# An attention and feed-forward layer on one Trainium2 core: rounds of two score pairs, and part of the softmax exponentials on VectorE

## The chip, the cores and the metric

The kernel runs on one core of one Trainium2 chip. Its engines are TensorE (PE in the profile; PEld is its weight load), ScalarE (ACT), VectorE (DVE), GpSimd (POOL) and SyncE (SP), which issues DMAs. The metric is the device time of one execution in microseconds (us), lower is better.

## The reference

The input is 4096 tokens of width 256. What is computed, cut to what matters:

```python
h = _layernorm(x) * (1 + ca) + sa
q = einsum('bnhd,hed->bnhe', h by 16 heads of 16, Wq)
attn = softmax(einsum('bnhe,bmhe->bhnm', q, q) / NORM)      # 16 heads of 4096 x 4096, NORM = 0.25
x = x + ga * (einsum('bhnm,bmhe->bnhe', attn, q) @ Wp.T + bp)
h = _layernorm(x) * (1 + cb) + sb
# feed-forward: a layer norm of its own, 256 -> 1024, silu, 1024 -> 256, dequantised weights
x = x + gb * _L0_ffn_ref(h, ...)                             # h + 0.5 * z
```

All scores are exponentiated: 16 x 4096 x 4096 of them.

## The kernel before

**Two stages.** The start stage (some 82 us) normalises the tokens, computes q, writes it to DRAM in two 16-bit parts and derives a shift for the softmax. The attend stage is nearly all of the time, and the change lies there.

**Tiling.** A block of tokens is 512 query tokens (eight blocks, `c`). A group is one block with 4 heads (four groups per block, 32 in all, `gg`). In a group there are 64 score pairs: 16 steps (`j`) by 4 heads, where a pair is two key tiles of 128 against the 512 queries. TensorE writes the scores of a pair, 128 x 1024, into one of three PSUM slots (`S_RING`); ScalarE takes their exp in one instruction (L744) and writes it into one of 12 buffers `probs` (`P_RING`). A score pair may be written when the exp of three pairs before has been done (semaphore `exps_done`).

**Weighing.** A unit is one key tile of four heads: four matmuls side by side of the `probs` against `values` (L788, function `weigh`), added up in the PSUM bank `ps_sums`. A group has 32 units. The matmuls of a unit are fp32 and are recorded as eight, in two passes of four. When a group is done, VectorE copies the sums (`copy_sums`, L927), TensorE turns them (`turn_sums`, L802), and VectorE divides (`divide`, L933 and L938). The first unit of the next group waits for that division (`group_done`).

**Output stage.** From group 4 on, TensorE also works on the block of tokens before: 44 pieces of work for a block (`out_piece`), 11 in each group: turning the attention result, the projection, turning the normalised tokens, the layer up (`up`, two pieces for each of 8 tiles of the hidden layer) and the layer down. All of them go through the one PSUM bank `ps_out`. After some pieces VectorE empties the bank (`after_piece`: `take_att`, `residual`, `take_z2`, `take_up` at L991, `finish_y`), and the next piece waits for it. A tile of the hidden layer needs a tanh on ScalarE (L729) and one more pass on VectorE (L995, `finish_hidden`). The two layer norms of a block run on VectorE in one go (`first_norm`, `second_norm`) while TensorE has no pieces that need them. GpSimd adds the bias to the tokens (L708) and makes the base of the output (L715 to L719).

**Order.** The order on each engine is written by hand. TensorE works in rounds (`SIZES`): ten of three score pairs, one of two, and again, 22 in a group. After the scores of a round come one or two units (`UNITS`), and in every second round one piece (`PLACE_ROUND`), so that a round holds two blocks of fp32 work: two units, or a unit and a piece. At a group's start, round 0 weighs the last two units of the group before and round 1 turns its sums. SyncE reloads a ring of four quarters of keys as each is used up.

## Time and profile before

| | us |
|---|---|
| median of 3 runs | 2074.18 (2073.5 to 2074.28) |
| the profiled execution | 2074.52 |
| its span, first to last instruction | 2072.7 |
| TensorE busy | 1958.2 |
| ScalarE busy | 1966.9 |
| VectorE busy | 377.8 |
| GpSimd busy | 70.4 |
| mean granted clock of TensorE | 0.993 |

The span is 1.8 us shorter than the profiled execution's own time, which is within 0.4 us of the median. A matmul's end in the profile is modelled and matmuls are pipelined, so a matmul's duration is longer than what it adds; what it adds is read from start to start. The same holds for ScalarE, whose instructions overlap a little. "issue" in a row is time without a wait that the profile shows.

### The profile page before, as it was taken

The numbers are of one execution on the slowest core, as the hardware profiler recorded it, in microseconds if no ns is written. First come the engines' busy times: TensorE is split into PE (matmuls) and PEld (weight loads), VectorE is DVE, ScalarE is ACT, GpSimd is POOL, SyncE is SP. The second block draws the span as 40 slices with busy tenths as digits, with TensorE's granted clock in tenths as the row PEclk, the third lists the DMA queues.
The fourth block names the chain that finished last, engine by engine and source line by source line (L and its number), as shares of the span: only waits on it lengthen the run. The fifth ranks groups of instructions, "written<-read, shape, count | busy, mean of one in ns | idle before, by whom it ended". The sixth has DMA issues, their size and how long they took to land.

```text
span 2072.7 us, 42098 instructions
## 1 busy us (share of the span) xinstructions
PE 1958.2 (94%) x18325; PEld 533.5 (26%) x18325; DVE 377.8 (18%) x903; ACT 1966.9 (95%) x2174; POOL 70.4 (3%) x35
## 2 busy tenths in 40 slices
PE   5888889999999999999999999999999999999997
PEld 4311112222222222222222222222222222222224
DVE  7310002210031100410022100311004100231004
ACT  3899999999999999999999999999999999999982
POOL 0000000100010000100001000100001000010000
PEclk9999999999999999999999999999999999999998
DMA  5541111211111221111211111111111112111100
GB/s 160 150 124 46 35 50 41 51 51 42 55 38 48 51 50 51 46 45 41 56 46 50 51 43 53 37 49 51 51 51 45 46 41 56 46 41 41 31 12 12
DMA packets 121337, 108.05 MB, mean 52 GB/s; under 512 B 21936, under 2 KB 120112, under 8 KB 120896
## 3 DMA queue, kind: packets, MB, share of 16 engines
q1 hardware_dynamic: 120400, 103.69, 18.8%
q8 instruction: 144, 2.36, 0.5%
q10 hardware_dynamic: 752, 1.67, 0.2%
q14 instruction: 41, 0.34, 0.1%
HBM read 96.49 MB, written 8.65 MB: 51 GB/s over the span
## 4 chain that ended last, share of the span: by engine, by line
ACT 46%; PE 42%; issue 7%; DVE 1%; ACTq 0%; DVEq 0%
ACT attend_probs L744 45%; PE attend_sums L788 21%; PE attend_scores L776 13%; PE attend_out L796 6%; PE attend_scores L796 1%; PE attend_out L802 1%; PE attend_sums L802 1%; ACT attend_half_tanh L729 1%; ACT attend_ffn_in L753 0%; PE attend_scores L802 0%; DVE attend_st L1085 0%; DVE z L1097 0%; DVE attend_rsqrt_work L91 0%; DVE attend_rsqrt_work L93 0%; DVE attend_rs L95 0%
## 5 line engine op out<-in xcount | busy, mean ns | idle before, releaser
L744 ACT ACTIVATE attend_probs<-attend_scores 128x1024 f32<-128x1024 f32 x2048 | 1891.6, 1038 | 18.6 <-PE attend_scores L776 18.6
L788 PE MATMUL attend_sums<-attend_probs,values 128*17 128x512 f32 x8192 | 1011.2, 597 | 0.0
L776 PE MATMUL attend_scores<-asks,keys 64*128 64x512 f16 x4096 | 673.3, 384 | 74.1 <-ACT attend_probs L744 57.4
L776 PEld LDWEIGHTS attend_scores<-asks,keys 64*128 64x128 f16 x4096 | 150.9, 94 | 886.0 <-ACT attend_probs L744 817.2
L788 PEld LDWEIGHTS attend_sums<-attend_probs,values 128*17 128x17 f32 x8192 | 171.3, 96 | 392.4 <-issue 337.3
L796 PE MATMUL attend_out<-w,hidden 128*32 128x256 f32 x1920 | 124.2, 379 | 0.0
L796 PE MATMUL attend_out<-attend_ffn_in,w 128*32 128x512 f32 x896 | 116.6, 592 | 0.0
L927 DVE COPY attend_sums_sb<-attend_sums 128x512 f32<-128x512 f32 x32 | 22.2, 692 | 487.4 <-PE attend_sums L788 487.4
L991 DVE TENSOR_SCALAR attend_half_in<-attend_out,b_col 128x512 f32<-128x512 f32 x56 | 42.0, 751 | 333.4 <-PE attend_out L796 332.4
L796 PEld LDWEIGHTS attend_out<-w,hidden 128*32 128x32 f32 x1920 | 62.0, 110 | 86.3 <-issue 64.2
L1001 DVE TENSOR_TENSOR base<-attend_out,base 128x512 f32<-128x512 f32 x14 | 9.7, 691 | 376.6 <-PE attend_out L796 376.6
L995 DVE SCALAR_TENSOR_TENSOR hidden<-attend_half_tanh,attend_half_in 128x512 f32<-128x512 f32 x56 | 38.8, 692 | 158.7 <-ACT attend_half_tanh L729 158.7
L715 POOL TENSOR_TENSOR base<-attend_hid,mod 128x1024 f32<-128x1024 f32 x7 | 16.6, 2368 | 1030.3 <-DVE attend_hid L977 1030.3
L708 POOL TENSOR_TENSOR attend_x_now<-attend_x_now,bp_ga 128x1024 f32<-128x1024 f32 x8 | 19.1, 2385 | 815.3 <-DMA attend_x_now<-L_attn_x 667.8
L796 PEld LDWEIGHTS attend_out<-attend_ffn_in,w 128*32 128x32 f32 x896 | 28.8, 110 | 59.9 <-issue 59.9
L729 ACT ACTIVATE attend_half_tanh<-attend_half_in 128x512 f32<-128x512 f32 x56 | 36.1, 644 | 0.0
L950 DVE TENSOR_TENSOR attend_x<-attend_out,attend_x_now 128x512 f32<-128x512 f32 x15 | 10.4, 691 | 140.9 <-PE attend_out L796 140.9
L802 PE MATMUL attend_sums<-ident,attend_sums_sb 128*32 128x128 f32 x1024 | 34.6, 276 | 0.8 <-DVE attend_sums_sb L927 0.8
L337 ACT ACTIVATE start_h_feat<-start_ps,mod_col 128x512 f32<-128x512 f32 x16 | 11.5, 773 | 22.8 <-PE start_ps L385 22.8
L796 PE MATMUL attend_out<-wp,attend_att_feat 128*32 128x256 f32 x480 | 31.2, 379 | 0.0
L753 ACT ACTIVATE attend_ffn_in<-attend_scores,beta_col,gamma_col 128x256 f32<-128x256 f32 x4 | 2.0, 560 | 29.6 <-PE attend_scores L796 29.6
L802 PEld LDWEIGHTS attend_sums<-ident,attend_sums_sb 128*32 128x32 f32 x1024 | 26.0, 109 | 8.8 <-DVE attend_sums_sb L927 8.8
(140 smaller groups left out, 548.2 us busy)
## 6 DMA issues: line engine op xcount, KB each, us to landing
keys<-parts_dram SPq DMA_DIRECT2D x768, 64.0 KB
keys<-parts_dram SPq DMA_DIRECT2D x256, 56.0 KB
asks<-parts_dram SPq DMA_DIRECT2D x192, 64.0 KB
start_x_in<-L_attn_x SPq DMA_DIRECT2D x8, 512.0 KB, 9.5
parts_dram<-start_q_parts SPq DMA_DIRECT2D x16, 256.0 KB, 2.5
attend_x_now<-L_attn_x SPq DMA_DIRECT2D x8, 512.0 KB, 4.3
out<-base SPq DMA_DIRECT2D x16, 256.0 KB, 2.7
asks<-parts_dram SPq DMA_DIRECT2D x64, 56.0 KB
```

Source lines behind the costliest of these rows:

```text
L337: last = act.activation(h_feat[:, g % 2, k, :], ps_turn[:, k, :], ACT.Identity, bias=mod_col[:, k:k + 1], scale=mod_col[:, 2 + k:3 + k])
L708: pool.tensor_tensor(x_now, x_now, wide(bp_ga[:, :]), ALU.add).then_inc(xb_ready, 1)
L715: pool.tensor_tensor(base, hid, wide(mod[:, 3, :]), ALU.mult).then_inc(base_step, 1)
L729: act.activation(half_tanh[:, f % 2, :], half_in[:, f % 2, :], ACT.Tanh).then_inc(tanh_done, 1)
L744: act.activation(probs[n % P_RING], ps_scores[:, 2 * slot:2 * slot + 2, :], ACT.Exp, scale=scale)\
L776: last = pe.matmul(ps_scores[:, 2 * (n % S_RING) + b, :], keys[rows, part % K_RING, hq, col:col + P], asks[rows, group * Q_HEADS + hq, :], ...
L788: last = pe.matmul(ps_sums[32 * hq:32 * hq + E1, :], values[:, j + STEPS * b, (gg % Q_GROUPS) * Q_HEADS + hq, :], probs[n % P_RING][:, b, ...
L796: last = pe.matmul(to[32 * q:32 * q + 32, :], held[:, 32 * q:32 * q + 32], moved, start=start, stop=stop)
L802: last = pe.matmul(bank[32 * q:32 * q + 32, t * P:(t + 1) * P], source(t)[:, 32 * q:32 * q + 32], ident[:, :], start=True, stop=True)
L927: dve.tensor_copy(sums_sb, ps_sums).then_inc(sums_copied, 1)
L991: dve.tensor_scalar(half_in[:, f % 2, :], ps_out, b1_col[:, f:f + 1], 0.5, ALU.add, ALU.mult).then_inc(half_ready, 1)
L995: dve.scalar_tensor_tensor(out=hidden[:, f, :], in0=half_tanh[:, f % 2, :], scalar=1.0, in1=half_in[:, f % 2, :], op0=ALU.add, op1=ALU.mul ...
```

## The change

**TensorE.** Rounds now have two score pairs each, 32 in a group. A round has one unit (rounds 9 and 21 have two, rounds 0 and 1 one each of the group before, rounds 2 and 3 none) and, in 22 of the 32 rounds, half a piece: half the query columns of the layer up, one tile of the hidden layer in the layer down, half of the tiles in a turn, one half of the contraction in the projection. The work in matmuls is the same. The sums are turned in round 2, the new group's weighing starts in round 4.

**Exps on VectorE.** In every seventh round (every fifth in the first four groups, with some left out) the first pair is a pair that lies 12 places ahead, and its exp is computed by VectorE in seven passes over 128 x 1024 (`exp_of`): the scores times 2^23/ln 2 as an integer, its fraction and its power of two by bit operations, and a product of two polynomials. It is written into one of two buffers `exps`. The passes are put into four rounds in a row: 0 and 1, then 2 and 3, then 4 and 5, then 6. The score slot is free after pass 0 (semaphore `taken`). That is 23 pairs in the first four groups and 114 in the other 28, 137 of 2048.

**GpSimd's work** goes to VectorE: four passes over 128 x 1024 for each block (`add_bias`, one in `second_norm`, `finish_base`). To make room in SBUF, `x_now` and `hid` share the space of `x1` and `z1`; the load of the next tokens is issued in the last quarter but one of a block's last group, after `finish_base`.

```diff
-SIZES = [3] * 10 + [2] + [3] * 10 + [2]
-ENDS = [sum(SIZES[:r + 1]) for r in range(len(SIZES))]
-STARTS = [0] + ENDS[:-1]
-UNITS = [0, 0] + [2 - r % 2 for r in range(2, len(SIZES))]
-WEIGHED = [sum(UNITS[:r + 1]) for r in range(len(SIZES))]
-PLACE_ROUND = range(1, len(SIZES), 2)
+ROUND = 2
+ROUNDS = PAIRS // ROUND
+LATE = 2
+UNITS = [0] * 4 + [2 if r in (9, 21) else 1 for r in range(4, ROUNDS)]
+WEIGHED = [sum(UNITS[:r + 1]) for r in range(ROUNDS)]
+PLACE_ROUND = [r for r in range(2, ROUNDS) if r % 4 != 1][:22]
...
+LEAD, E_RING = 12, 2
+def vector_round(gg, r):
+    if gg < Q_GROUPS:
+        return (ROUNDS * gg + r) % 5 == 0 and (gg != 1 or r < 15)
+    busy = gg % Q_GROUPS == 0 and 15 <= r <= 28
+    return (ROUNDS * gg + r) % 7 == 0 and not busy
+def emission():
+    order, by_vector, taken, following = [], [], set(), 0
+    for gg in range(GROUPS):
+        for r in range(ROUNDS):
+            for i in range(ROUND):
+                early = len(order) + LEAD
+                if i == 0 and vector_round(gg, r) and early < GROUPS * PAIRS and early not in taken:
+                    order.append(early)
+                    by_vector.append(True)
+                    taken.add(early)
+                    continue
+                while following in taken:
+                    following += 1
+                order.append(following)
+                by_vector.append(False)
+                taken.add(following)
+    return order, by_vector
+ORDER, BY_VECTOR = emission()
+PLACE = {n: e for e, n in enumerate(ORDER)}
+TURN = [sum(BY_VECTOR[:e]) if BY_VECTOR[e] else e - sum(BY_VECTOR[:e]) for e in range(len(ORDER))]
+SCALAR_PAIRS = [n for n, v in zip(ORDER, BY_VECTOR) if not v]
+VECTOR_PAIRS = [n for n, v in zip(ORDER, BY_VECTOR) if v]
...
+TURN_ATT, PROJECT, TURN_Z2, UP, DOWN = 0, 2, 10, 12, 28
...
+                dve.tensor_scalar(log2_scale, exp_scale, 2.0 ** 23 / math.log(2.0), None, ALU.mult).then_inc(scale_set, 1)
...
+        hid = z2 = z1[:, :, :]
...
+            eng.dma_start(x1, x_v[:, o * GT:(o + 1) * GT, :]).then_inc(xn_in, 16)
...
-                    if within == 8 and c > 0:
-                        sp.wait_ge(x1_ready, 2 * c)
+                    if within == 14 and c > 0:
+                        sp.wait_ge(base_step, 3 * c)
...
-            @block.gpsimd
...
-                    pool.tensor_tensor(x_now, x_now, wide(bp_ga[:, :]), ALU.add).then_inc(xb_ready, 1)
...
+                        if not BY_VECTOR[e]:
+                            turn, slot = TURN[e], e % S_RING
+                            act.wait_ge(scores_ready, e + 1)
+                            if turn >= P_RING:
+                                act.wait_ge(steps_done, SCALAR_PAIRS[turn - P_RING] // Q_HEADS + 1)
+                            act.activation(probs[turn % P_RING], ps_scores[:, 2 * slot:2 * slot + 2, :], ACT.Exp, scale=scale)\
+                               .then_inc(exps_done, 1)
...
+                    if e >= S_RING:
+                        pe.wait_ge(taken if BY_VECTOR[e - S_RING] else exps_done, TURN[e - S_RING] + 1)
...
+                        wait(pe, vector_exps, before(VECTOR_PAIRS, gg * PAIRS + Q_HEADS * (j + 1)))
...
+                def up(f, k, half, bank):
+                    cols = slice(half * D, (half + 1) * D)
+                    last = by_columns(bank[:, cols], w1[:, k, f * P:(f + 1) * P], ffn_in[:, k, cols], k == 0, k == DC - 1)
+                    if k == DC - 1 and half == 1:
...
-                    for r in range(len(SIZES)):
-                        for p in range(STARTS[r], ENDS[r]):
-                            scores(gg, p)
-                        if r == 0 and gg > 0:
-                            for unit in range(WEIGHED[-1], 2 * STEPS):
-                                weigh(gg - 1, unit)
-                        if r == 1 and gg > 0:
-                            turn_sums(gg - 1)
+                    for r in range(ROUNDS):
+                        for p in range(ROUND * r, ROUND * r + ROUND):
+                            scores(gg * PAIRS + p)
+                        if r < LATE and gg > 0:
+                            weigh(gg - 1, WEIGHED[-1] + r)
                         for unit in range(WEIGHED[r] - UNITS[r], WEIGHED[r]):
                             weigh(gg, unit)
                         if r in PLACE_ROUND and c > 0:
-                            out_piece(c - 1, group * SLOTS + r // 2)
+                            out_half(c - 1, group * SLOTS + PLACE_ROUND.index(r))
+                        if r == LATE and gg > 0:
+                            turn_sums(gg - 1)
...
+                def add_bias(o):
+                    dve.wait_ge(xn_in, 16 * (o + 1))
+                    dve.tensor_tensor(x1, x1, wide(bp_ga[:, :]), ALU.add).then_inc(xb_ready, 1)
+                def finish_base(o):
+                    dve.wait_ge(base_step, 3 * o + 1)
+                    dve.tensor_tensor(base, base, wide(b2_gb[:, :]), ALU.add).then_inc(base_step, 1)
+                    dve.wait_ge(base_step, 3 * o + 2)
+                    dve.tensor_tensor(base, base, x1, ALU.add).then_inc(base_step, 1)
+                def exp_of(d, i):
+                    e = PLACE[VECTOR_PAIRS[d]]
+                    slot, values_out = e % S_RING, exps[d % E_RING].rearrange("p b n -> p (b n)")
+                    power_f = power.bitcast(F32)
+                    if i == 0:
+                        dve.wait_ge(scores_ready, e + 1)
+                        wait(dve, exp_scaled, d)
+                        if d == 0:
+                            dve.wait_ge(scale_set, 1)
+                        dve.tensor_scalar(power, ps_scores[:, 2 * slot:2 * slot + 2, :].rearrange("p b n -> p (b n)"),
+                                          log2_scale, -120.0 * 2.0 ** 23, ALU.mult, ALU.max).then_inc(taken, 1)
+                    elif i == 1:
+                        dve.wait_ge(taken, d + 1)
+                        wait(dve, vector_exps, d)
+                        dve.tensor_scalar(fraction.bitcast(I32), power, 0x007FFFFF, 0x3E800000,
+                                          ALU.bitwise_and, ALU.bitwise_or).then_inc(power_step, 1)
+                    elif i == 2:
+                        dve.wait_ge(power_step, 4 * d + 1)
+                        dve.tensor_scalar(power, power, 0x7F800000, FACTOR,
+                                          ALU.bitwise_and, ALU.bitwise_xor).then_inc(power_step, 1)
+                    elif i == 3:
+                        dve.wait_ge(power_step, 4 * d + 2)
+                        if d >= E_RING:
+                            dve.wait_ge(steps_done, VECTOR_PAIRS[d - E_RING] // Q_HEADS + 1)
+                        dve.scalar_tensor_tensor(out=values_out, in0=fraction, scalar=A1 * 2.0 ** -2, in1=fraction,
+                                                 op0=ALU.add, op1=ALU.mult).then_inc(power_step, 1)
+                    elif i == 4:
+                        dve.wait_ge(power_step, 4 * d + 3)
+                        dve.scalar_tensor_tensor(out=fraction, in0=fraction, scalar=B1 * 2.0 ** -2, in1=fraction,
+                                                 op0=ALU.add, op1=ALU.mult).then_inc(power_step, 1)
+                    elif i == 5:
+                        dve.wait_ge(power_step, 4 * d + 4)
+                        dve.scalar_tensor_tensor(out=fraction, in0=fraction, scalar=B0 * 2.0 ** -4, in1=power_f,
+                                                 op0=ALU.add, op1=ALU.mult).then_inc(exp_scaled, 1)
+                    elif i == 6:
+                        dve.wait_ge(exp_scaled, d + 1)
+                        dve.scalar_tensor_tensor(out=values_out, in0=values_out, scalar=A0 * 2.0 ** -4, in1=fraction,
+                                                 op0=ALU.add, op1=ALU.mult).then_inc(vector_exps, 1)
...
-                    if gg > 0:
-                        copy_sums(gg - 1)
-                        divide(gg - 1)
-                    if gg == 1:
-                        weights()
-                    if gg == 2:
-                        gate_weights()
-                    if c > 0:
-                        for s in range(group * SLOTS, (group + 1) * SLOTS):
-                            after_piece(c - 1, s)
-                            after_tanh(c - 1, s)
+                    for r in range(ROUNDS):
+                        now = ROUNDS * gg + r
+                        if r - 1 in PLACE_ROUND and c > 0:
+                            h = group * SLOTS + PLACE_ROUND.index(r - 1)
+                            if h % 2 == 1:
+                                after_piece(c - 1, h // 2)
+                        if BY_VECTOR[ROUND * now]:
+                            begun_at[now] = begun
+                            begun += 1
+                            for i in (0, 1):
+                                exp_of(begun_at[now], i)
+                        if r == LATE and gg > 0:
+                            copy_sums(gg - 1)
+                        if r == LATE + 1 and gg > 0:
+                            divide(gg - 1)
+                        for ago, steps in ((1, (2, 3)), (2, (4, 5)), (3, (6,))):
+                            if now - ago in begun_at:
+                                for i in steps:
+                                    exp_of(begun_at[now - ago], i)
+                        if r - 3 in PLACE_ROUND and c > 0:
+                            h = group * SLOTS + PLACE_ROUND.index(r - 3)
+                            if h % 2 == 1:
+                                after_tanh(c - 1, h // 2)
+                        if (gg, r) == (1, 18):
+                            weights()
+                        if (gg, r) == (1, 24):
+                            gate_weights()
+                        if (group, r) == (0, 5) and c > 0:
+                            add_bias(c - 1)
+                        if (group, r) == (2, 13) and c > 0:
+                            finish_base(c - 1)
...
+                add_bias(G - 1)
```

**TensorE, inside a token block's layer up.** Before; L776 scores, L788 a unit, L796 a piece:

```order
L776 MATMUL attend_scores<-asks,keys 128x512 [waits exps_done]
L776 MATMUL attend_scores<-asks,keys 128x512
L776 MATMUL attend_scores<-asks,keys 128x512 [waits exps_done]
L776 MATMUL attend_scores<-asks,keys 128x512
L776 MATMUL attend_scores<-asks,keys 128x512 [waits exps_done]
L776 MATMUL attend_scores<-asks,keys 128x512
L788 MATMUL attend_sums<-attend_probs,values 17x512 x4
L796 MATMUL attend_out<-attend_ffn_in,w 32x512 [waits half_ready]
L796 MATMUL attend_out<-attend_ffn_in,w 32x512 x3
L776 MATMUL attend_scores<-asks,keys 128x512 [waits exps_done]
```

and of the changed kernel (L826 scores, L839 a unit, L847 half a piece; `attend_exps` is a pair of VectorE's):

```order
L826 MATMUL attend_scores<-asks,keys 128x512 [waits exps_done]
L826 MATMUL attend_scores<-asks,keys 128x512
L826 MATMUL attend_scores<-asks,keys 128x512 [waits exps_done]
L826 MATMUL attend_scores<-asks,keys 128x512
L839 MATMUL attend_sums<-attend_exps,values 17x512 [waits vector_exps,exps_done]
L839 MATMUL attend_sums<-attend_probs,values 17x512 x3
L847 MATMUL attend_out<-attend_ffn_in,w 32x256 [waits half_ready]
L847 MATMUL attend_out<-attend_ffn_in,w 32x256 x3
L826 MATMUL attend_scores<-asks,keys 128x512 [waits exps_done]
L826 MATMUL attend_scores<-asks,keys 128x512
L826 MATMUL attend_scores<-asks,keys 128x512 [waits exps_done]
L826 MATMUL attend_scores<-asks,keys 128x512
```

The piece has become two of 256 columns, in two rounds, and each stands behind two pairs and one unit.

**VectorE, at the start of group 10**, where the sums are copied and divided. Before:

```order
L995 SCALAR_TENSOR_TENSOR hidden<-attend_half_tanh,attend_half_in 128x512
L927 COPY attend_sums_sb<-attend_sums 128x512
L933 RECIPROCAL attend_inverse<-attend_sums 128x16
L938 TENSOR_TENSOR attend_att<-attend_sums,attend_inverse 128x4x64
L991 TENSOR_SCALAR attend_half_in<-attend_out,b_col 128x512
```

and of the changed kernel, where L1065 and L1070 are passes 0 and 1 of an exp and L985 is the copy of the sums:

```order
L1106 SCALAR_TENSOR_TENSOR hidden<-attend_half_tanh,attend_half_in 128x512
L1065 TENSOR_SCALAR attend_power<-attend_scores,gains 128x1024
L1070 TENSOR_SCALAR attend_fraction<-attend_power 128x1024
L985 COPY attend_sums_sb<-attend_sums 128x512
L991 RECIPROCAL attend_inverse<-attend_sums 128x16
L996 TENSOR_TENSOR attend_att<-attend_sums,attend_inverse 128x4x64
L1074 TENSOR_SCALAR attend_power<-attend_power 128x1024
L1080 SCALAR_TENSOR_TENSOR attend_exps<-attend_fraction 128x1024
L1084 SCALAR_TENSOR_TENSOR attend_fraction<-attend_fraction 128x1024
L1088 SCALAR_TENSOR_TENSOR attend_fraction<-attend_fraction,attend_power 128x1024
```

Two passes of an exp, which wait for scores of round 2, now stand ahead of the copy, and the other five behind the division.

## Rows read from the trace of the kernel before

**Rows 1.** Page, part 1: busy time, share of the span and instructions of each engine.

```profile
PE 1958.2 (94%) x18325; PEld 533.5 (26%) x18325; DVE 377.8 (18%) x903; ACT 1966.9 (95%) x2174; POOL 70.4 (3%) x35
```

**Rows 2.** Busy time per stretch: groups 1 to 3, then groups 4 to 7.

```profile
core 0: us, PE busy (x) PEld busy (x) DVE busy (x) ACT busy (x) POOL busy (x), PEclk, DMA share, GB/s
143.50:319.70 176.20, 156.93 (x1248) 34.17 (x1248) 14.73 (x23) 176.20 (x194) 2.49 (x1) 1.00 0.17 45
319.70:561.70 242.00, 235.91 (x2242) 61.27 (x2242) 39.69 (x86) 239.79 (x266) 9.51 (x4) 1.00 0.18 47
```

**Rows 3.** Timeline, PE: a round with one unit and a piece (start us, us).

```profile
1004.67 0.99 PE L776 MATMUL attend_scores<-asks,keys 64*128 64x512 f16 x6
1005.59 1.05 PE L788 MATMUL attend_sums<-attend_probs,values 128*17 128x512 f32 x8
1006.46 1.05 PE L796 MATMUL attend_out<-w,hidden 128*32 128x256 f32 x16
1007.44 0.60 PE L776 MATMUL attend_scores<-asks,keys 64*128 64x512 f16 x4
```

**Rows 4.** Timeline, PE: second of three score pairs in that round.

```profile
1004.90 0.38 PE L776 MATMUL attend_scores<-asks,keys 64*128 64x512 f16 x2
```

**Rows 5.** Timeline, PEld: third score pair and unit of that round.

```profile
1005.27 0.10 PEld L776 LDWEIGHTS attend_scores<-asks,keys 64*128 64x128 f16 x2 [0.48 <-ACT attend_probs L744]
1005.59 0.13 PEld L788 LDWEIGHTS attend_sums<-attend_probs,values 128*17 128x17 f32 x8 [0.23 <-issue]
```

**Rows 6.** Timeline, PE: a group boundary, sums turned.

```profile
1047.85 1.14 PE L776 MATMUL attend_scores<-asks,keys 64*128 64x512 f16 x6
1048.91 1.08 PE L802 MATMUL attend_sums<-ident,attend_sums_sb 128*32 128x128 f32 x32
1049.81 1.06 PE L802 MATMUL attend_out<-ident,attend_att 128*32 128x128 f32 x32
```

**Rows 7.** Timeline, ACT: an exp, a tanh and the next exp.

```profile
448.30 1.03 ACT L744 ACTIVATE attend_probs<-attend_scores 128x1024 f32<-128x1024 f32 x1
449.20 0.64 ACT L729 ACTIVATE attend_half_tanh<-attend_half_in 128x512 f32<-128x512 f32 x1
449.72 1.03 ACT L744 ACTIVATE attend_probs<-attend_scores 128x1024 f32<-128x1024 f32 x1
```

**Rows 8.** Timeline, ACT: an exp that came after an idle wait for its scores.

```profile
501.80 1.02 ACT L744 ACTIVATE attend_probs<-attend_scores 128x1024 f32<-128x1024 f32 x1 [0.44 <-PE attend_scores L776]
```

**Rows 9.** Timeline, PE: the scores that it waited for.

```profile
501.37 0.82 PE L776 MATMUL attend_scores<-asks,keys 64*128 64x512 f16 x6
```

**Rows 10.** Timeline, DVE: sums copied and divided at that boundary.

```profile
1047.98 0.69 DVE L927 COPY attend_sums_sb<-attend_sums 128x512 f32<-128x512 f32 x1 [1.90 <-PE attend_sums L788]
1050.06 0.26 DVE L933 RECIPROCAL attend_inverse<-attend_sums 128x16 f32<-128x16 f32 x1 [1.39 <-PE attend_sums L802]
1050.35 0.42 DVE L938 TENSOR_TENSOR attend_att<-attend_sums,attend_inverse 128x256 f32<-128x256 f32 x1
```

**Rows 11.** Groups by line, DVE: operations like the added ones (mean ns).

```profile
L991 DVE TENSOR_SCALAR attend_half_in<-attend_out,b_col 128x512 f32<-128x512 f32 x56 | 42.0, 751 | 333.4 <-PE attend_out L796 332.4
L977 DVE TENSOR_TENSOR attend_hid<-attend_hid,mod 128x1024 f32<-128x1024 f32 x7 | 8.6, 1226 | 0.2
```

**Rows 12.** Groups by line, DVE, 60 to 420 us: SBUF to SBUF, constant operands.

```profile
L1029 DVE TENSOR_SCALAR z<-mod 128x512 f32<-128x512 f32 x1 | 0.4, 415 | 0.0
```

**Rows 13.** Timeline, DVE: two passes after each other, and the second norm's end.

```profile
835.97 0.69 DVE L950 TENSOR_TENSOR attend_x<-attend_out,attend_x_now 128x512 f32<-128x512 f32 x1 [9.80 <-PE attend_out L796]
842.35 1.23 DVE L975 TENSOR_TENSOR attend_hid<-z,mod 128x1024 f32<-128x1024 f32 x1
843.61 1.23 DVE L977 TENSOR_TENSOR attend_hid<-attend_hid,mod 128x1024 f32<-128x1024 f32 x1
853.65 1.38 DVE L981 TENSOR_SCALAR z<-attend_hid,attend_mo,attend_rs 128x256 f32<-128x256 f32 x4
```

**Rows 14.** Timeline, DVE: in its first work of the attend stage.

```profile
83.59 0.68 DVE L1033 TENSOR_TENSOR z<-z,mod 128x512 f32<-128x512 f32 x1
```

168 lines of the change are left out of this document (85 added, 83 removed).

## The prediction

> **What bounds the kernel now.** I read the page's busy times first: ScalarE 95%, TensorE 94% [rows 1]. With two engines that near to full, shares decide nothing, and the stretches come next. Groups 1 to 3, without an output stage, take 176.2 us for 192 score pairs, or 0.918 a pair: ScalarE is busy all of it, TensorE for 156.93, so ScalarE is the bound. A token block with the output stage (groups 4 to 7) takes 242.0 us, 60.5 a group, and there TensorE is busy for 235.91 and ScalarE for 239.79 [rows 2]. So in 28 of 32 groups TensorE is nearly as late as ScalarE, and each engine has to be costed from start to start, since durations overlap.
>
> *TensorE.* From one score pair to the next 0.23 [rows 3, 4]. From the last pair of a round to the unit 0.32 [rows 5], so going over to fp32 work costs 0.09. A unit takes 0.87 (1005.59 to 1006.46). From the piece to the next scores 0.98; the piece itself has as many columns as a unit, 0.86, so going back costs 0.12 [rows 3]. Each round thus pays 0.21 for changing over and back, whatever lies between. A turn of the sums takes 0.90 [rows 6]. A group's own work, before: 64 x 0.23 = 14.7, 32 units at 0.87 = 27.8, 11 pieces at 0.86 = 9.5, the turn 0.9, and 22 rounds x 0.21 = 4.6: **57.5 us** of 60.5.
>
> *ScalarE.* 0.90 from an exp to the next when its work is ready, 0.52 for a tanh between two exps [rows 7]. A group with two tanhs: 64 x 0.90 + 2 x 0.52 = 58.6; the remaining 1.9 are waits for scores or buffers such as the 0.44 of [rows 8].
>
> **The change, part by part.**
>
> *Rounds of two.* The same matmuls, but 32 rounds: ten more changes over and back, 10 x 0.21 = **+2.1**. TensorE's own work becomes **59.6 us** a group; it was 60.5 in all. That TensorE pays for the change of form and not for the size of the blocks is what these rows show. The Trainium skill has a rule that speaks against this change (TensorEngine Tiling (Array Packing), Key Properties): changing the tiling mode drains the engine, changing the tile alone does not. Scores use the array in two halves of 64 rows and the fp32 work in groups of 32 columns. By that rule the 0.21 is a drain that comes each time; were it only the latency of a wait, TensorE's own work would be 57.5 less 4.6, whatever the rounds, which is the third rival.
>
> *Exps taken from ScalarE.* 114 pairs in 28 groups, 4.1 a group: 4.1 x 0.90 = 3.7 less, ScalarE's own 58.6 becomes 54.9. From group 4 on this buys at most the way down to TensorE's 59.6: 60.5 - 59.6 = 0.9 a group. **ScalarE stops being the bound, TensorE becomes it**, and every wait of TensorE then counts in full.
>
> *What an exp costs on VectorE.* Pass 0 reads PSUM: 0.75 for 512 elements, and 512 more cost 1.23 - 0.69 = 0.54 [rows 10, 11], so 1.29. Passes 1 and 2 have one source in SBUF and constants: 0.415 for 512 [rows 12], twice that less the fixed 0.16, so 0.67. No row shows a bit operation of that size; the upper end is 1.23, that of a two-source pass, and I take 0.67, the nearer row. Passes 3 to 6: 1.23 each [rows 11]. 0.03 between dependent passes [rows 13]. Passes 0-1: 1.99; 2-3: 1.96; 4-5: 2.52; 6: 1.26: **7.7 us in a row**, of some 13 us between two such exps, so VectorE has the time but not at every moment. The skill (VectorE: DVE Perf Modes, What auto-detection actually checks) lets the operands decide on the faster mode and not the operation; by it, 0.67 too, and only if that fails here 1.23.
>
> Pass 0 starts as an exp does, 0.43 after its scores [rows 8, 9], so passes 0-1 end 2.42 after the start of the round. A full round is 0.23 + 0.32 + 0.87 + 0.43 + 0.12 = 1.96, one without half a piece 1.53.
>
> *The copy of the sums.* It began 0.13 after the next scores (1047.98, 1047.85) and lasts 0.69 [rows 6, 10]; with 0.06 to reach TensorE it ends 0.88 into round 2, and the turn is due at 0.23 + 0.32 + 0.43 = 0.98. The spare is 0.10. An exp of VectorE comes every seven rounds, so one always lies near the boundary, by round:
> - 2: passes 0-1 stand ahead of the copy, free at 2.42: TensorE waits 2.2
> - 1: 2.42 - 1.53 = 0.89: waits 0.7
> - 0: with passes 2-3, 4.38 - 3.06 = 1.32: 1.1
> - 31: with passes 4-5, 6.90 - 4.59 = 2.31: 2.1
> - 30: with pass 6, 8.16 - 6.55 = 1.61: 1.4
> - 3: the copy is in time, but the division (0.26 + 0.42) stands behind passes 0-1 and ends at 3.2; round 4's unit wants it at 1.10 + 0.55: 1.6
> - 29: 0.
>
> The mean of the seven is **1.3 a group**. Queued behind the waiting turn or unit are all scores, so ScalarE starves behind it.
>
> *The bank `ps_out`.* After an emptying piece VectorE's pass (0.69 to 0.75) is done 0.94 into the next round and wanted at 1.42. If the exp began three rounds before, passes 4-5 end at 6.90 - 5.88 = 1.02, the pass at 1.86: a wait of 0.4, and 0.9 with a short round among the three; at two or four rounds 0.3 to 0.4, only with short rounds. Over the seven positions 0.2 for each of some 14 such places in a block: 2.8, or **0.7 a group**.
>
> *Other waits.* The score slot: passes 0-1 begun at 0.43, `taken` at 1.78, wanted 0.23 into the next round, 2.19, or 1.76 behind a short round, later when `take_up` stands ahead: 0.2. ScalarE: in rounds 29, 31, 0, 1, 5 TensorE needs 1.53 and in round 3 only 1.10, against 1.80 for two exps, and a tanh adds 0.52, so TensorE waits for exps there; between 0 and 2.5, and I take 0.7, since VectorE's exp or a wait above often falls on the same rounds.
>
> From group 4 on: 59.6 + 1.3 + 0.7 + 0.2 + 0.7 = 62.5, against 60.5: **+2.0 x 28 = +56 us**; nothing of it lies beside other work, as TensorE is the path.
>
> *The first four groups.* TensorE's own work there is 59.6 - 9.5 = 50.1 and ScalarE stays the bound: 23 pairs x 0.918 = -21. Against it: an exp every five rounds (nine of ScalarE's, 8.3 us) leaves 0.6 beside the 7.7, three boundaries cost some 2 each, and the first pair of all goes to VectorE, which was still on its first work at 83.59 [rows 14], some 2 to 3 late. **-12 us.**
>
> *At nothing.* GpSimd's work moved: 4 x 1.23 = 4.9 a block on VectorE, in rounds without an exp near it except `finish_base` (2.5), which can delay a `taken` by 1 once in several blocks. The norms ran from 835.97 to 855.0 [rows 13], 19 us, within 11 rounds of at least 1.9; one pass more still fits. SyncE's load waits for `finish_base`, two thirds of a group earlier; stores and keys behind it have 30 us. The tail and the start stage keep their chains (+0.2 for one small pass).
>
> **The sum.** 2074.5 + 56 - 12 = 2118.5. The terms of the waits were taken one by one though they partly fall together, which takes off a little: **2116 us**, 2% slower.
>
> **The rivals.**
>
> *VectorE is never late* (a wait falls where ScalarE would have made TensorE wait anyway). Then 59.6 + 0.9 = 60.5 from group 4 on, no change, and the first groups give 21 less some 4: some 2056, and with the waits for ScalarE at half, 2045. For it: VectorE is 18% busy and gets 137 x 7.5 = 1030 us more, half of the span. Against: the copy's spare of 0.10. It would need the boundary waits below 0.5 a group. Faster.
>
> *The bit operations take the slow mode*: 1.12 more in each chain, 8.8 of 8.3 us available in the first groups (VectorE is the bound there, +12), and each case above later by 0.56 to 1.12: +1.2 at the boundary and in `ps_out` together: +34. Some 2162. Against: the rows of the same form.
>
> *The changes over and back are hidden*: then TensorE's own work is 52.9, ScalarE stays the bound with 54.9 and waits of about 2.5, so 57.5: -3.0 x 28 - 12, some 1978. Against: the 0.32 and 0.98 stand in rounds where TensorE was not held.
>
> *The change doesn't do what it says*: ScalarE's exps would still be 2048. The order on the engines excludes it.
>
> **Chances.** The forecast 0.64 (2085 to 2145), VectorE in time or nearly so 0.20 (2040 to 2085, of which 0.14 lies below 2070 and 0.04 within 0.2% of before), slow bit operations 0.10, changes hidden 0.04, others 0.02. 0.2%, 4 us, is about what a measurement of this kernel can tell from no change. Faster 0.18, same 0.06, slower 0.76. The range of 2050 to 2145 leaves out the slow bit operations, the hidden changes and the lowest part of the second case, some 0.2.
>
> **What the profile would show.** TensorE: 1.95 to 1.97 from round to round and 0.32 ahead of each unit. The exps on ScalarE: 1911, with idle time ahead of them that names scores. Waits of TensorE that name VectorE: the turn for the copy (some 1 us a group), `ps_out` work for L1102, scores for L1065. VectorE's passes: 1.29, 0.67, 0.67, 4 x 1.23. Groups 1 to 3 at 54 to 56 us, later ones at 62 to 63. I am wrong if the later groups take 60.5 or less, which would mean that the waits for VectorE fall together with those for ScalarE, or that a round costs TensorE less than 1.96.

## The result and the profile after

The changed kernel takes 2242.66 us (median of 4 runs, 2242.02 to 2244.17) beside 2073.84 of before: **8.2% slower**, ratio 1.0815 with an interval of 1.0796 to 1.0834. The direction was as forecast, the size was not: 169 us lost instead of 42.

The page of the changed kernel (columns as in [rows 1]):

```profile
PE 1969.9 (88%) x19221; PEld 512.3 (23%) x19221; DVE 1385.0 (62%) x1885; ACT 1890.4 (84%) x2038; POOL 1.3 (0%) x6
```

No engine is near full: TensorE has gone from 94% to 88%, ScalarE from 95% to 84%. GpSimd is empty, VectorE at 62%. VectorE computes 136 exps (x136 in its rows below; ScalarE's are x1912 of 2048), one fewer than the 137 that the section on the change and the prediction give. A token block with the output stage, groups 4 to 7 (columns as in [rows 2]):

```profile
core 0: us, PE busy (x) PEld busy (x) DVE busy (x) ACT busy (x) POOL busy (x), PEclk, DMA share, GB/s
326.50:587.20 260.70, 237.09 (x2372) 58.83 (x2368) 159.07 (x204) 231.26 (x248) 0.00 (x0) 1.00 0.17 44
```

It takes 260.7 us where it took 242.0 [rows 2], 65.2 a group. TensorE is busy for as long as before (237.09 against 235.91); what has been added is idle time of TensorE. Who it waited for, from the waits of the changed kernel (line waited: us in total, times, longest):

```profile
PE attend_sums L839 <- ACT attend_probs L788: 162.5, 179, 1.8
PE attend_sums L853 <- DVE attend_sums_sb L985: 19.6, 22, 1.9
PE attend_sums L839 <- DVE attend_exps L1092: 8.3, 1, 8.3
PE attend_scores L826 <- DVE attend_power L1065: 7.1, 12, 3.3
PE attend_sums L839 <- DVE attend_att L996: 4.8, 5, 1.0
PE attend_scores L826 <- ACT attend_probs L788: 4.6, 15, 0.7
PE attend_out L847 <- DVE attend_half_in L1102: 4.1, 6, 1.1
```

The rows with DVE are, but for one, the waits that the prediction was about, at the turn of the sums, the score slots, the first unit and the output bank, and they are small. The one is the single wait of 8.3 us for the last pass of an exp (L1092), which the prediction did not have. **The first row is the result**: TensorE waited 162.5 us, 179 times, ahead of a unit of weighing (L839) for an exp of ScalarE. The kernel before has no such row for TensorE's matmuls at all. Read from start to start, which also counts the part that the profile hides under the modelled end of a matmul and takes in the units that waited for VectorE, units come 187.5 us later in all than the usual 0.32 after their scores, at 191 places (those later by more than 0.1); before, at one place, by 0.2.

One of these places, at the end of group 21. TensorE (start us, us; L826 scores, L839 a unit, L847 half a piece):

```profile
1503.84 0.60 PE L826 MATMUL attend_scores<-asks,keys 64*128 64x512 f16 x4
1505.66 1.05 PE L839 MATMUL attend_sums<-attend_probs,values 128*17 128x512 f32 x8 [1.21 <-ACT attend_probs L788]
1506.53 0.61 PE L847 MATMUL attend_out<-attend_ffn_in,w 128*32 128x256 f32 x8
1507.08 0.61 PE L826 MATMUL attend_scores<-asks,keys 64*128 64x512 f16 x4
...
1508.60 0.61 PE L826 MATMUL attend_scores<-asks,keys 64*128 64x512 f16 x4
1510.93 1.05 PE L839 MATMUL attend_sums<-attend_probs,values 128*17 128x512 f32 x8 [1.73 <-ACT attend_probs L788]
```

and ScalarE:

```profile
1502.75 3.77 ACT L788 ACTIVATE attend_probs<-attend_scores 128x1024 f32<-128x1024 f32 x4 [0.71 <-PE attend_scores L826]
1507.51 1.03 ACT L788 ACTIVATE attend_probs<-attend_scores 128x1024 f32<-128x1024 f32 x1 [0.98 <-PE attend_scores L826]
```

The scores of round 30 start at 1503.84, and the unit that should follow 0.32 later starts at 1505.66. ScalarE's four exps of the first row take 3.77, the last of them 1.03, so they start some 0.91 apart. The third, at about 1504.6, is the exp of the pair issued at 1503.84; it ends at about 1505.6, and the unit starts then. **The unit waits for the exp of a pair of its own round.** Until it is through, TensorE issues no scores, so ScalarE then stands idle for 0.98 in its turn. The unit at 1510.93 is the same again, one round after the group's end, with a tanh in between: 1.73 of idle time.

**Why so close.** A unit number u (0 to 31) of even u needs the pairs up to 2u + 3 of its group, one of odd u those up to 2u + 1. In rounds 4 to 8 the unit of round r is r - 4; behind the double round 9 it is r - 3, behind the double round 21 it is r - 2. So the unit of round 22, number 20, needs pair 43, which in the natural order is the second of round 21, the last pair issued before the unit's own round. And an early pair in the order pushes each pair behind it one place back until its own turn comes 12 places on, which with one every 14 places is most of the time. Then pair 43 is the first pair of round 22 itself. The order comes this close in rounds 22, 24, 26, 28 and 30 and in round 0 of the next group, six places a group.

Worked through `ORDER` and `UNITS` for the whole kernel and held against the starts in the trace:

| the last pair that the unit needs | places | late | late by, us in all |
|---|---|---|---|
| in the unit's own round | 129 | 129 | 149.3, or 1.16 each |
| second pair of the round before | 78 | 50 | 31.7, of which 8.3 are the wait for L1092 |
| further back | 751 | 12 | 6.5, nine of them at the first unit of a group, behind the division |

So every unit that needs a pair of its own round is late, and these 129 places hold four fifths of the lateness.

### The profile page after: what moved, and what is told of

The parts are those of the page before. It is cut to its first block, busy times and chain, and to the rows that moved or that the text cites. A ratio compares the mean times of both kernels' runs of the same rounds, so it can differ in the third digit from the quotient of the medians.

```text
span 2240.2 us, 46970 instructions
## 1 busy us (share of the span) xinstructions
PE 1969.9 (88%) x19221; PEld 512.3 (23%) x19221; DVE 1385.0 (62%) x1885; ACT 1890.4 (84%) x2038; POOL 1.3 (0%) x6
## 4 chain that ended last, share of the span: by engine, by line
PE 54%; ACT 18%; issue 12%; DVE 11%; ACTq 0%; DVEq 0%
PE attend_sums L839 29%; ACT attend_probs L788 18%; PE attend_scores L826 14%; PE attend_out L847 8%; DVE attend_power L1065 2%; DVE attend_exps L1080 1%; PE attend_scores L847 1%; DVE attend_fraction L1084 1%; DVE attend_fraction L1088 1%; DVE attend_fraction L1070 1%; PE attend_sums L853 1%; DVE attend_power L1074 1%; PE attend_out L853 1%; DVE attend_exps L1092 1%; DVE attend_sums_sb L985 1%
## 5 line engine op out<-in xcount | busy, mean ns | idle before, releaser
L788 ACT ACTIVATE attend_probs<-attend_scores 128x1024 f32<-128x1024 f32 x1912 | 1813.4, 1040 | 259.8 <-PE attend_scores L826 255.1
L839 PE MATMUL attend_sums<-attend_probs,values 128*17 128x512 f32 x7648 | 1066.3, 598 | 148.0 <-ACT attend_probs L788 142.8
L826 PE MATMUL attend_scores<-asks,keys 64*128 64x512 f16 x4096 | 642.3, 384 | 21.0 <-DVE attend_power L1065 7.1
L1065 DVE TENSOR_SCALAR attend_power<-attend_scores,gains 128x1024 int32<-128x1024 f32 x136 | 174.4, 1282 | 483.0 <-PE attend_scores L826 462.8
L839 PE MATMUL attend_sums<-attend_exps,values 128*17 128x512 f32 x544 | 280.3, 600 | 27.9 <-ACT attend_probs L788 19.7
L826 PEld LDWEIGHTS attend_scores<-asks,keys 64*128 64x128 f16 x4096 | 132.4, 94 | 669.4 <-ACT attend_probs L788 411.5
L839 PEld LDWEIGHTS attend_sums<-attend_probs,values 128*17 128x17 f32 x7648 | 141.4, 95 | 521.0 <-issue 257.3
L1080 DVE SCALAR_TENSOR_TENSOR attend_exps<-attend_fraction 128x1024 f32<-128x1024 f32 x136 | 166.6, 1225 | 5.7 <-PE attend_sums L839 1.1
L1088 DVE SCALAR_TENSOR_TENSOR attend_fraction<-attend_fraction,attend_power 128x1024 f32<-128x1024 f32 x136 | 166.6, 1225 | 4.7
L1092 DVE SCALAR_TENSOR_TENSOR attend_exps<-attend_exps,attend_fraction 128x1024 f32<-128x1024 f32 x136 | 166.3, 1223 | 3.5
L1084 DVE SCALAR_TENSOR_TENSOR attend_fraction<-attend_fraction 128x1024 f32<-128x1024 f32 x136 | 166.2, 1222 | 3.5
L847 PE MATMUL attend_out<-w,hidden 128*32 128x256 f32 x1920 | 145.5, 381 | 1.1 <-DVE attend_half_in L1102 1.1
L847 PE MATMUL attend_out<-attend_ffn_in,w 128*32 128x256 f32 x1792 | 138.2, 380 | 5.9 <-DVE attend_half_in L1102 2.9
L1070 DVE TENSOR_SCALAR attend_fraction<-attend_power 128x1024 int32<-128x1024 int32 x136 | 94.3, 694 | 4.7
L1074 DVE TENSOR_SCALAR attend_power<-attend_power 128x1024 int32<-128x1024 int32 x136 | 94.0, 691 | 3.4
L847 PEld LDWEIGHTS attend_out<-w,hidden 128*32 128x32 f32 x1920 | 60.6, 110 | 138.9 <-issue 133.4
L847 PEld LDWEIGHTS attend_out<-attend_ffn_in,w 128*32 128x32 f32 x1792 | 55.3, 110 | 143.6 <-issue 124.6
L853 PE MATMUL attend_sums<-ident,attend_sums_sb 128*32 128x128 f32 x1024 | 35.8, 282 | 19.6 <-DVE attend_sums_sb L985 19.6
L839 PEld LDWEIGHTS attend_sums<-attend_exps,values 128*17 128x17 f32 x544 | 32.3, 95 | 83.3 <-issue 43.9
```

What stands on the lines that cost most here:

```text
L788: act.activation(probs[turn % P_RING], ps_scores[:, 2 * slot:2 * slot + 2, :], ACT.Exp, scale=scale)\
L826: last = pe.matmul(ps_scores[:, 2 * (e % S_RING) + b, :], keys[rows, part % K_RING, hq, col:col + P], asks[rows, group * Q_HEADS + hq, :], ...
L839: last = pe.matmul(ps_sums[32 * hq:32 * hq + E1, :], values[:, j + STEPS * b, (gg % Q_GROUPS) * Q_HEADS + hq, :], held(n)[:, b, :], start= ...
L847: last = pe.matmul(to[32 * q:32 * q + 32, :], held[:, 32 * q:32 * q + 32], moved, start=start, stop=stop)
L853: last = pe.matmul(bank[32 * q:32 * q + 32, t * P:(t + 1) * P], source(t)[:, 32 * q:32 * q + 32], ident[:, :], start=True, stop=True)
L1065: dve.tensor_scalar(power, ps_scores[:, 2 * slot:2 * slot + 2, :].rearrange("p b n -> p (b n)"), log2_scale, -120.0 * 2.0 ** 23, ALU.mult, ...
```

## The experiments

Each was timed beside the kernel before on the same chip.

**e1: the two double units late.** The edit:

```diff
-UNITS = [0] * 4 + [2 if r in (9, 21) else 1 for r in range(4, ROUNDS)]
+UNITS = [0] * 4 + [2 if r in (29, 31) else 1 for r in range(4, ROUNDS)]
```

> The changed kernel with one number pair changed: the two rounds with two units are 29 and 31, no longer 9 and 21, so each unit from round 9 on stands one or two rounds later behind its scores. Theory W (the time went into units that wait for exps of pairs issued just before them; 187 us of such waits in the trace of the changed kernel, none before): these waits fall to some 30 us, and the time by 130 to 2110 us. Rival D (VectorE is late for the copy of the sums, the output bank and the score slots, and my sizes for that were too small): those places are as before, so about 2240 us, at most 10 less.

2112.43 us (2111.56 to 2113.85), ratio 1.0184 (1.0167 to 1.0201). The changed kernel lost **130 us less by one pair of numbers**, with the same instructions on every engine. Its waits of TensorE:

```profile
PE attend_sums L839 <- ACT attend_probs L788: 22.0, 24, 1.8
PE attend_sums L853 <- DVE attend_sums_sb L985: 16.8, 20, 1.9
```

The wait for exps has gone from 162.5 to 22.0 us; the wait for the copy of the sums, VectorE's, was 19.6 and is 16.8. The block of groups 4 to 7 takes 247.0 us, 61.8 a group:

```profile
310.80:557.80 247.00, 239.04 (x2372) 59.97 (x2368) 158.99 (x204) 230.00 (x249) 0.00 (x0) 0.99 0.18 46
```

Theory W (units too close behind their scores) stands, rival D (VectorE's lateness, larger than I had it) falls. The order of the pairs is the same; with the double units late, the last pair needed is in the unit's own round at 23 places where it was 129, all 23 in round 0, and all 23 are late, by 1.0 us each. That is the wait that is left.

**e2: no exps on VectorE.**

```diff
 def vector_round(gg, r):
+    return False
```

> Rounds of two and half pieces as changed, but all exps on ScalarE and all pairs in their natural order; GpSimd's work stays on VectorE. Theory W: without the early pairs each unit's pairs stand one place earlier, so the waits ahead of the units fall from 187 to some 45 us, though ScalarE has all exps again: about 2090 us, above the 2074 of before, since rounds of two cost TensorE 2.1 us more per group and units 18 and later still stand close behind their pairs. Rival D gives the waits for VectorE back and makes ScalarE the bound again: about 2075 us. If a round of two itself cost more than I read, it would stay above 2150.

2091.07 us (2090.5 to 2093.82), ratio 1.0085 (1.0068 to 1.0102). The unit's wait is still there, smaller and shorter each time (0.4 on average where it was 0.9), since nothing pushes the pairs back. By the order no unit needs a pair of its own round; 191 need the last of the round before, and 131 of them are late, by 0.42 on average:

```profile
PE attend_sums L840 <- ACT attend_probs L789: 46.2, 125, 0.8
```

**e3: the order alone.** The early pairs stay in the order, but ScalarE does their exps as well, into three buffers of their own where VectorE had two.

```diff
-LEAD, E_RING = 12, 2
+LEAD, E_RING = 12, 3
...
+                        else:
+                            turn, slot = TURN[e], e % S_RING
+                            act.wait_ge(scores_ready, e + 1)
...
+                            act.activation(exps[turn % E_RING], ps_scores[:, 2 * slot:2 * slot + 2, :], ACT.Exp, scale=scale)\
+                               .then_inc(vector_exps, 1)
...
-                        pe.wait_ge(taken if BY_VECTOR[e - S_RING] else exps_done, TURN[e - S_RING] + 1)
+                        pe.wait_ge(vector_exps if BY_VECTOR[e - S_RING] else exps_done, TURN[e - S_RING] + 1)
...
-                                    exp_of(begun_at[now - ago], i)
+                                    pass
```

> The changed kernel's order of pairs, the early pairs included, but ScalarE does their exps too (into three buffers of their own, where the changed kernel has two); VectorE has none of the passes. Theory W: the early pair pushes every following pair one place back towards its unit, whoever does the exp, so the waits ahead of the units stay near 180 us and the time near 2205 us. Rival D: with VectorE free the waits go, about 2075 to 2090 us.

2214.01 us (2211.58 to 2216.41), ratio 1.0675 (1.0657 to 1.0693). VectorE is back at 17% and all exps are on ScalarE, as in e2, yet it is 123 us slower than e2. TensorE's waits ahead of units and ahead of the turn:

```profile
PE attend_sums L844 <- ACT attend_probs L786: 176.1, 184, 2.1
PE attend_sums L858 <- DVE attend_sums_sb L990: 1.7, 4, 0.8
```

With the double units in rounds 9 and 21, nearly three quarters of the loss against the kernel before come from putting 136 pairs 12 places ahead, **whoever computes them**: 123 of the 152 us between e2 and the changed kernel are there.

**e4: two of the seven passes.** Passes 1 to 5 are left out and pass 6 is a short one that writes a constant, so VectorE's pairs carry no exps.

```diff
-                    elif i == 1:
-                        dve.wait_ge(taken, d + 1)
...
                     elif i == 6:
+                        dve.wait_ge(taken, d + 1)
...
+                        dve.tensor_scalar(values_out, fraction, 1.0, None, ALU.mult).then_inc(vector_exps, 1)
```

> Of the seven passes of each of VectorE's exps only pass 0 and one short last pass are left, so VectorE's pairs get a constant in place of their exps; order, rounds and waits are as changed. VectorE has some 5.8 us less per such pair. Theory W: only the waits for VectorE at the copy and in the output bank fall, some 45 us: about 2195 us. Rival D: nearly all of the loss comes back, 2090 us or less.

2205.44 us (2204.12 to 2206.9), ratio 1.0631 (1.0613 to 1.0649): with most of VectorE's new work gone, 37 of 169 us come back.

**e9: the same, double units late.** e4's edit and e1's. It leaves out the same passes.

> e1 (double units late, VectorE's exps as in the changed kernel) with passes 1 to 5 of each of VectorE's exps left out, so VectorE's pairs get a constant. With the waits ahead of the units mostly gone, what is left against e1 is VectorE's lateness at the copy, the division and the output bank, which the prediction put at 2.0 us a group from group 4 on: 56 us less at most, theory W's round-by-round sum says 48, so 2064 us. If those waits are hidden behind others as in the rival of the prediction: less than 20 us, 2095 or more.

2073.25 us (2070.96 to 2075.15), ratio 0.9998 (0.9989 to 1.0007). Against e1 that is **39 us for VectorE's lateness**, expected 48; it is what five of the seven passes cost, as pass 0 and the short one (0.69 us) are still there. The wait for exps has not moved, the one for the copy has:

```profile
PE attend_sums L839 <- ACT attend_probs L788: 22.0, 24, 1.8
PE attend_sums L853 <- DVE attend_sums_sb L985: 6.2, 8, 1.2
```

**e5: rounds of two by themselves.** e2's edit and e1's: no exps on VectorE, natural order, double units late.

> All exps on ScalarE in natural order, rounds of two and half pieces, and the double units in rounds 29 and 31: what rounds of two cost by themselves, without waits ahead of the units. TensorE's own work is 2.1 us a group above before's, but still below ScalarE's pace with its waits (60.5 a group), so theory W says the time of before within 5 us, about 2071 us. If a round of two cost more than its changes over and back, or halving the pieces cost something, it would be 2090 or more.

2075.87 us (2073.27 to 2077.62), ratio 1.0006 (0.9996 to 1.0015): no difference that can be measured, 5 us above what I wrote. The units' waits for exps are gone from the profile; what TensorE waits for is again the exp ahead of the next scores (57.4 us in the kernel before):

```profile
PE attend_scores L827 <- ACT attend_probs L789: 24.0, 76, 0.5
```

So ScalarE's pace sets the time again. Rounds of two and half pieces cost nothing as long as ScalarE is the bound.

**e6: no exp of VectorE near a group's boundary.** e1 with other rounds from group 4 on:

```diff
-    return (ROUNDS * gg + r) % 7 == 0 and not busy
+    return r in (4, 11, 18, 25) and not busy
```

> As e1 (double units in rounds 29 and 31), but from group 4 on VectorE's rounds are 4, 11, 18 and 25 of each group (4 and 11 in a block's first group), so that none stands near the copy and the division of the sums: 121 exps on VectorE where e1 has 137. The boundary term of the prediction (1.1 to 1.3 us a group) and the last waits ahead of units should go: 1.8 us a group, about 2062 us against e1's 2112. If the waits at the boundary do not matter, 2100 or more.

2064.3 us (2062.57 to 2067.21), ratio 0.9954 (0.994 to 0.9967). With 121 exps on VectorE where e1 has 136, 48 us less:

```profile
PE attend_sums L839 <- ACT attend_probs L788: 3.9, 4, 1.8
PE attend_sums L853 <- DVE attend_sums_sb L985: 2.3, 4, 0.9
```

The copy's wait falls from 16.8 to 2.3, the unit's from 22.0 to 3.9. The unit's wait is the order's: with these rounds the last pair needed is in the unit's own round at 3 places, where e1 has 23. The copy's wait is VectorE's, as e9 shows, where it fell from 16.8 to 6.2 and the unit's stayed at 22.0. How the 48 us divide between the two, and what the 15 exps fewer did, this run cannot tell.

**e7: exps on VectorE in the first groups only.** e5 with

```diff
-        return (ROUNDS * gg + r) % 5 == 0 and (gg != 1 or r < 15)
+        return r in (4, 9, 14, 19, 24) and gg + r > 4 and (gg != 1 or r < 15)
...
-    return (ROUNDS * gg + r) % 7 == 0 and not busy
+    return False
```

> As e5, with exps on VectorE in the first four groups alone (17 of them, in rounds 4, 9, 14, 19 and 24), where there is no output stage and ScalarE is the bound: 17 x 0.9 = 15 us less than e5, about 2056 us, faster than before.

2061.73 us (2059.45 to 2063.36), ratio 0.9934 (0.992 to 0.9947), 14 less than e5: 0.83 for each of 17 exps, where ScalarE's own pace is 0.90. Expected was 2056; the step down was right, the start of it (e5) was not.

**e8: exps placed where TensorE waits for them.** e7, and from group 4 on

```diff
-    return False
+    return r in ((), (4, 10, 15, 20), (7, 18), (4,))[gg % Q_GROUPS]
```

> As e7, and from group 4 on VectorE has exps only where TensorE waits for ScalarE and no copy, division or emptying of the output bank is due: rounds 4, 10, 15, 20 of a block's second group, 7 and 18 of its third, 4 of its fourth (66 in all). Each takes away a wait of TensorE for an exp: 0.6 us a group more, about 2039 us. If any exp on VectorE from group 4 on costs TensorE more than it gives, it is slower than e7.

2041.09 us (2040.24 to 2042.7), ratio **0.9841** (0.9828 to 0.9855). This beats the kernel before by 33 us. The page and the block of groups 4 to 7:

```profile
PE 1959.9 (96%) x19221; PEld 524.9 (26%) x19221; DVE 868.4 (43%) x1395; ACT 1922.1 (94%) x2108; POOL 1.3 (0%) x6
304.40:543.70 239.30, 236.36 (x2372) 60.53 (x2368) 91.92 (x139) 235.77 (x258) 0.00 (x0) 1.00 0.19 48
```

239.3 us, 59.8 a group, with TensorE at 96% of the span. TensorE's matmuls have no wait ahead of a unit in the profile, and by the order no unit needs a pair of its own round. The 49 exps from group 4 on gave 21 us, 0.42 each, half of ScalarE's 0.90. That TensorE's own work comes next and takes the other half is likely by the 59.8, but no run shows it apart.

**e10: e8 with the double units early.** e1's edit undone.

> e8 with the double units back in rounds 9 and 21. Theory W: the only difference is how close units stand behind their scores, and e8's 66 exps push the pairs one place back for about 60% of the time, so the waits ahead of the units come back with some 90 us: about 2125 us. If the place of the double units mattered only through something else of the changed kernel (VectorE's chain every seven rounds), e8's 2041 would hardly move.

2120.63 us (2119.79 to 2121.95), ratio 1.0226 (1.0212 to 1.024): 80 us above e8 by the same two numbers, with VectorE busy for 41% of the span.

```profile
PE attend_sums L839 <- ACT attend_probs L788: 92.1, 155, 1.7
```

By the order 50 units now need a pair of their own round, and all 50 are late, by 1.15 us each. How far a unit stands behind its scores decides, not VectorE's load.

The four corners, double units by early pairs (us):

| | no early pairs | as in the change |
|---|---|---|
| double units in rounds 9 and 21 | 2091 (e2) | 2243 (the change) |
| double units in rounds 29 and 31 | 2076 (e5) | 2112 (e1) |

Each alone costs 15 or 37 us, both together 167. The places at which a unit needs a pair of its own round are 0 (e2), 0 (e5), 23 (e1) and 129 (the change): a pair pushed one place back does little until the unit stands one round behind it. The right column also has the exps on VectorE; without five of their seven passes the 37 are gone (e9, 2073).

## Why the prediction was wrong

**Rounds of two on TensorE: right.** The 0.21 for each change over and back gave 59.6 us of own work a group. A block of e5, which has no exp on VectorE, keeps the time of before (242 us), and e8 comes down to 59.8 a group and no further, at 96% busy. The rival in which the changes over are hidden is out: in the rows of the changed kernel above, the half piece at 1506.53 and the next scores at 1507.08 stand 0.55 apart, 0.43 of work and 0.12 for the change back. The prediction held against that rival that TensorE was not held in the rounds read; in its rows 5 the third pair had waited 0.48 for an exp, so that round proved less than it said. Over the whole changed kernel the unit follows its scores by 0.31 in the median.

**The cost of an exp on VectorE: right.** 1.29, 0.67, 0.67 and 1.23 were forecast; the groups of the changed kernel (mean ns of one):

```profile
L1065 DVE TENSOR_SCALAR attend_power<-attend_scores,gains 128x1024 int32<-128x1024 f32 x136 | 174.4, 1282 | 483.0 <-PE attend_scores L826 462.8 <-issue 20.1
L1070 DVE TENSOR_SCALAR attend_fraction<-attend_power 128x1024 int32<-128x1024 int32 x136 | 94.3, 694 | 4.7
L1074 DVE TENSOR_SCALAR attend_power<-attend_power 128x1024 int32<-128x1024 int32 x136 | 94.0, 691 | 3.4
L1080 DVE SCALAR_TENSOR_TENSOR attend_exps<-attend_fraction 128x1024 f32<-128x1024 f32 x136 | 166.6, 1225 | 5.7 <-PE attend_sums L839 1.1
```

The bit operations take the fast mode, 0.69, so that rival is out too.

**VectorE's lateness: right in kind, too large.** The prediction had 1.3 for the boundary and 0.7 for the output bank, 2.0 a group or 56 us; e9 against e1 shows 39 us in all 32 groups, e4 against the change 37, each for five of the seven passes. Why it was less is not shown. The cases of the boundary were worked out one by one with TensorE on time in each round, and where it is late for another reason VectorE could catch up; but in e1, where TensorE is late far less often, the wait for the copy was no longer than in the changed kernel (16.8 against 19.6). The rival in which VectorE is never late is refuted by the same two pairs of runs, though with the double units late and the passes gone the time (e9) is no better than before's.

**The term that was missing: units that wait for exps.** The step that failed is the paragraph on other waits, and with it the 62.5 a group. The prediction lists whom TensorE waits for ahead of scores, the turn, a group's first unit and the output bank, and takes every other unit as ready, 0.87 after 0.32, in each round: it put that wait at nothing without a reason. The groups took 65.2. The semaphore of the unit stood in the order's rows (`waits vector_exps,exps_done`), `UNITS` and `emission` stood in the diff, and I never worked out which pair the unit of round 22 needs. It is the last one of the round before, or with an early pair outstanding the first of the unit's own round. From that pair's scores to its exp's end there are 0.43 + 1.03 us and, when another exp stands in line, up to 0.9 more; in its own round the order leaves 0.23 + 0.32 = 0.55. That is 0.9 to 1.8 late, and the 129 such units were 1.16 late on average. e1 puts what the double units' place adds to that term at 130 us. Added to the forecast of 2116 with VectorE's lateness at 39 in place of 56, it gives 2229, 14 short of the measured time.

Those 14 are not closed. Four things bear on them: the wait that e1 still has ahead of units (22.0 us in the profile); TensorE's waits for exps ahead of scores, for which the prediction took 0.7 a group, some 20 us, and which were 4.6; the wait for L1092 below; and TensorE's mean granted clock, 0.989 where it was 0.993, by an estimate from these two at most some 10 us. Idle times and differences between runs do not add up exactly, so they are not put into a sum here. That e1 came within 4 us of the forecast is in part luck: it still has the 22 us that the forecast left out, and VectorE's lateness in it is 17 less.

**One term put at nothing was not.** In group 28 the last pass of an exp stands on VectorE behind the block's two norms, and the unit of round 22 waits for it:

```profile
1954.84 1.22 DVE L1092 SCALAR_TENSOR_TENSOR attend_exps<-attend_exps,attend_fraction 128x1024 f32<-128x1024 f32 x1
1956.20 1.01 PE L839 MATMUL attend_sums<-attend_exps,values 128*17 128x512 f32 x1 [8.27 <-DVE attend_exps L1092]
```

The exp was begun in round 14, the last that `busy` lets through, and its pass before had ended at 1939.26. It is the only block in which an exp falls on that round. In e1 the same wait is 5.2 us. TensorE stood from 1947.9 to 1956.2, and from 1952.6 to 1959.4 its granted clock was 0.50, the lower of its two levels (1.2 GHz); it was 1.00 before and 0.99 behind.

**The first four groups** were forecast 12 us faster; by the starts of the groups' scores they took 244 us where before took 237, with the same wait at work. In e1 they took 229, the forecast of 225 within 4.

**The range** left out all this, since its upper end came from the known terms only. No case stood for a wait that I had not costed.

## What to carry to other kernels

When a change alters the order or the spacing on a queue, work out for every wait of the queue's instructions which instruction it now needs and how many places back that stands, and not only for the waits that the change adds. Moving a few items forward pushes all others back: a consumer that ran one item behind its producer now meets it. And where a helper engine takes over work, its instructions belong where the bound engine waits anyway: with the double units late in both, 66 exps placed so gave 33 us against before (e8), 136 at even intervals lost 38 (e1).

## What the runs showed of the hardware

VectorE's tiny operations on 128 x 4 elements were slow in the kernel before when they began while GpSimd was at work on one of its 128 x 1024 passes, and are not in the changed kernel, where GpSimd does nothing. The same instruction in the kernel before and in the changed one:

```profile
L88 DVE TENSOR_SCALAR attend_rs<-attend_rsqrt_work 128x4 int32<-128x4 int32 x14 | 16.9, 1204 | 0.5
```

```profile
L141 DVE TENSOR_SCALAR attend_rs<-attend_rsqrt_work 128x4 int32<-128x4 int32 x14 | 2.4, 170 | 0.5
```

The mean is 1204 ns against 170. It mixes seven of some 2240, in the second norm, with seven of 170, in the first. One of the slow ones of before, and GpSimd's pass beside it:

```profile
847.55 2.24 DVE L88 TENSOR_SCALAR attend_rs<-attend_rsqrt_work 128x4 int32<-128x4 int32 x1
847.36 2.40 POOL L717 TENSOR_TENSOR base<-base,b_gb 128x1024 f32<-128x1024 f32 x1
```

It ends 0.03 us after the pass. All tiny operations of the two norms in the kernel before fit this: the 21 that began during a pass of GpSimd lasted 0.58 to 2.24 us and ended 0.02 to 0.03 after the pass; the 14 that began some 0.02 ahead of a pass and the 181 with no pass beside them took at most 0.17. So the operation is not slowed in proportion, it is held until the pass is over. Not every operation is: the four `BATCH_NORM_STATS2` and the four `BATCH_NORM_AGGREGATE` of the second norm, nearly all begun during a pass, took 1.41 and 0.38 us, and 1.40 and 0.38 in the changed kernel without one. The runs show the two together; no run takes GpSimd's work away alone, so that one holds the other is what these rows suggest, not more.

The work moved to VectorE there (four passes of 1.22 a block, where GpSimd took 2.4) costs no time that the runs show: e5, which has it, is level with before. The two norms, from the last residual on, took 19 us before and, with one pass more, 15.8 in the changed kernel (1939.17 to 1954.92).
